# Context keys of the last cross-attention made one layer earlier, subtractions eight tiles ahead, and slot logits multiplied once

## The reference

```python
x_n = l2norm(x_ln, -1) * scale
mu_n = l2norm(mu, 0)
logits = einsum('bnd,des->bnes', x_n, mu_n)
dispatch = softmax(logits, axis=1)
combine = softmax(logits.reshape(B, N, E * S), axis=-1)
slot_in = einsum('bnd,bnes->besd', x_ln, dispatch)
```

```python
q = rope(rms_norm(q, q_norm_w), draft_position_ids)
k = rope(rms_norm(k, k_norm_w), full_position_ids)
scores = einsum('bhqd,bhkd->bhqk', q, repeat(k)) * SCALE
attn = einsum('bhqk,bhkd->bhqd', softmax(scores), v)
```

## Time and profile before

| | |
|---|---|
| three executions | 1602.79, 1604.55, 1605.17 us; median 1604.55 |
| the profiled execution | 1604.83 us, its span 1603.1 us |
| PE busy | 1413.8 us (88%) |
| DVE busy | 1122.8 us (70%) |
| ACT busy | 868.8 us (54%) |
| POOL busy | 469.7 us (29%) |
| mean granted TensorE clock | 0.937 |
| slot experts | 543 to 630 us of the span |
| self-attention of the third layer | 708 to 756 us |
| last cross-attention | 770 to 1238 us |

### The profile page before, as it was taken

How to read it: one execution, slowest core, us unless ns; L and a number is a source line. 1 busy time by engine, 2 the same in 40 slices (tenths; PEclk the granted TensorE clock), 3 DMA queues, 4 the chain that set the end, 5 groups by cost and what they waited for, 6 DMA issues and landing times. The chain is left out here.

```text
span 1603.1 us, 23976 instructions
## 1 busy us (share of the span) xinstructions
PE 1413.8 (88%) x8072; PEld 993.9 (62%) x8072; DVE 1122.8 (70%) x2240; ACT 868.8 (54%) x2300; POOL 469.7 (29%) x515
## 2 busy tenths in 40 slices
PE   7876988867998789987779899999998989999969
PEld 5653444445775457876557677877777436666657
DVE  4687999825665555764559768766854679999953
ACT  2446989832124264426445445445554579999831
POOL 2244000000000001530447326534600037777710
PEclk9986999977999799998889899999999999999979
DMA  3002999965341402200200000000000453333120
GB/s 144 1 1 51 180 185 186 178 183 162 105 136 33 99 14 51 90 1 1 79 2 12 14 8 8 14 1 1 1 1 10 141 159 119 101 103 114 40 78 8
DMA packets 192390, 112.89 MB, mean 70 GB/s; under 512 B 150233, under 2 KB 166617, under 8 KB 191628
## 3 DMA queue, kind: packets, MB, share of 16 engines
q1 hardware_dynamic: 192268, 111.35, 26.7%
HBM read 77.51 MB, written 0.26 MB: 49 GB/s over the span
## 5 line engine op out<-in xcount | busy, mean ns | idle before, releaser
L672 DVE TENSOR_REDUCE x_row_max<-banks 128x1 f32<-128x512 f32 x248 | 152.7, 682 | 14.4 <-PE banks L366 14.3
L575 ACT ACTIVATE x_v_full<-banks,x_neg_max,x_q_scale 128x1024 int16<-128x1024 f32 x128 | 153.4, 1202 | 15.1 <-DMA x_v_full<-x_v_full 7.6
L212 PE MATMUL banks<-a_w_ring,x_normed_T 128*128 128x512 f32 x320 | 146.6, 598 | 4.8 <-DVE a_r L3193 4.8
L2389 PE MATMUL banks<-ctx_tokens,x_kT 128*128 128x512 f32 x272 | 139.8, 601 | 2.4 <-ACT ctx_tokens L2551 2.4
L2416 PEld LDWEIGHTS banks<-x_v,x_weights_T 128*128 128x128 f32 x896 | 111.2, 193 | 30.0 <-ACT x_weights_T L2567 15.9
L2416 PE MATMUL banks<-x_v,x_weights_T 128*128 128x129 f32 x896 | 118.8, 278 | 7.8 <-ACT x_weights_T L2567 7.8
L2505 POOL TENSOR_TENSOR ctx_tokens<-ctx_tokens 128x512 f32<-128x512 f32 (+1 forms) x48 | 71.4, 1487 | 136.6 <-DVE ctx_tokens L2655 136.6
L2674 DVE TENSOR_TENSOR ctx_tokens<-ctx_tokens,x_weights_T 128x512 f32<-128x512 f32 x104 | 88.3, 849 | 31.7 <-ACT x_weights_T L2557 31.2
L366 PE MATMUL banks<-x_kT_parts,x_qT_int 64*128 64x512 bf16 x512 | 103.5, 402 | 7.1 <-DVE x_row_max L672 3.5
L2684 DVE TENSOR_TENSOR x_weights_T<-x_weights_T,ctx_tokens 128x512 f32<-128x512 f32 x112 | 90.2, 829 | 24.8 <-ACT ctx_tokens L2563 24.7
L427 PEld LDWEIGHTS banks<-x_v_full,x_v_int 128*16 128x16 f16 x1024 | 57.2, 91 | 76.3 <-DMA x_v_full<-x_v_full 46.4
(11 more groups left out here) (532 smaller groups left out, 3374.4 us busy)
## 6 DMA issues: line engine op xcount, KB each, us to landing
a_w_ring<-in_L_attn_WB_T SPq DMA_DIRECT2D x16, 512.0 KB
a_w_ring<-in_L_attn_WC_T SPq DMA_DIRECT2D x16, 512.0 KB
f_w_gate_up<-in_L_ffn_gate_up SPq DMA_DIRECT2D x18, 352.0 KB
ctx_tokens<-in_ctx SPq DMA_DIRECT2D x16, 256.0 KB, 5.7
x_wq<-in_L_xattn_Wq_T SPq DMA_DIRECT2D x8, 512.0 KB, 3.7
a_w_ring<-in_L_attn_Wth_T SPq DMA_DIRECT2D x8, 512.0 KB
a_bias_ring<-in_L_attn_B_bias_perm SPq DMA_DIRECT2D x16, 256.0 KB
a_bias_ring<-in_L_attn_C_bias_perm SPq DMA_DIRECT2D x16, 256.0 KB
```

Of the source, the lines that this page charges most:

```text
L212: last = nc.tensor.matmul(out, lhsT, rhs, start=(i == 0), stop=(i == len(pairs) - 1))
L575: nc.scalar.activation(eb[:, q % RING], k.ps[:, 2 + 2 * (q % 2):4 + 2 * (q % 2), :].rearrange("p a n -> p (a n)"), ACT.Exp, bias=nb[:, v % ...
L672: nc.vector.reduce_max(mx[:, u % 2, i:i + 1], k.bank(MBANK[m % 3]), AX.X).then_inc(s.max_taken, 1)
L2389: nc.tensor.matmul(k.bank(s_bank(key)), kt[:, u % 2, j * P:(j + 1) * P], flat(qt[:, u % 2]), start=True, stop=True).then_inc(s.scores_in_p ...
```

## The change

In the slot experts the dispatch logits are no longer a product of their own: TensorE turns tiles of the scaled combine logits (`turn_logits`). Combine logits are therefore made in the order of column pieces, both batch elements of one piece before the next, and from piece 0 ahead of the loop; their exponentials go to a second buffer (`cexp`, in the place of `mu`), both in ScalarE's step 2, and the first products are spread over steps 1 and 2.

```diff
-ncol = sb("neg_mu_rnorm", [P, ne])
+cexp = k.mu[:].rearrange("p c s -> p (c s)").rearrange("p (b s) -> p b s", b=B)
...
     def combine_logits(n):
-        b, j = divmod(n, 4)
+        j, b = divmod(n, B)
+        if b == 0 and j == 0:
+            pe.wait_ge(s.xT_ready, B)
...
-    def dispatch_logits(p):
-        if p == 0:
-            pe.wait_ge(s.xT_ready, B)
-        else:
+    def turn_logits(p):
+        pe.wait_ge(s.logits_taken, B * (p // 2 + 1))
+        if p >= 1:
             pe.wait_ge(s.dexp_ready, 4 * p)
         for e in range(2):
             a = (2 * p + e) * SLOTS
-            last = matmul_acc(nc, k.bank(0, P, BT, e * BT), [(k.mu[:, c, a:a + SLOTS], xst[:, c]) for c in range(DC)])
+            for b in range(B):
+                last = nc.tensor.transpose(k.bank(0, P, P, (e * B + b) * T), comb[:, b, a:a + SLOTS], k.ident[:])
         last.then_inc(s.dlog_ready, 1)
...
         turn_x(b)
-    steps = ((0, dispatch_logits), (1, turn), (3, turn_combine), (2, hidden), (3, slot_out), (4, combine))
+    for n in range(4):
+        combine_logits(n)
+    steps = ((0, turn_logits), (1, turn), (3, turn_combine), (2, hidden), (3, slot_out), (4, combine))
     for i in range(NPAIR + 4):
         for lag, step in steps:
             if 0 <= i - lag < NPAIR:
                 step(i - lag)
-            if lag == 1 and i < 2:
-                for n in range(4 * i, 4 * i + 4):
+            if lag == 0 and i < 2:
+                for n in range(4 + 2 * i, 6 + 2 * i):
                     combine_logits(n)
-            if lag == 1 and i == 1:
-                for n in range(4):
+            if lag == 1 and i in (1, 2):
+                for n in range(2 * i - 2, 2 * i):
                     first_product(n)
...
                 nc.scalar.activation(disp[:, r, e, b], k.bank(0, P, T, (e * B + b) * T), ACT.Exp, bias=dm[:, r, 1, e, b:b + 1],
-                                     scale=k.mu_col[:, 2 * p + e:2 * p + e + 1], accum_out=dm[:, r, 2, e, b:b + 1]).then_inc(s.dexp_ready, 1)
+                                     accum_out=dm[:, r, 2, e, b:b + 1]).then_inc(s.dexp_ready, 1)
 
     def combine_exps(b):
         act.wait_ge(s.cmax_ready, b + 1)
-        nc.scalar.activation(comb[:, b], comb[:, b], ACT.Exp, bias=sm[:, b, 4:5], accum_out=sm[:, b, 5:6]).then_inc(s.cexp_ready, 1)
+        nc.scalar.activation(cexp[:, b], comb[:, b], ACT.Exp, bias=sm[:, b, 4:5], accum_out=sm[:, b, 5:6]).then_inc(s.cexp_ready, 1)
...
-            combine_exps(i - 1)
-        if i == 1:
-            for n in range(4):
+            for n in range(2 * i - 2, 2 * i):
                 take_product(n)
+        if i == 2:
+            for b in range(B):
+                combine_exps(b)
         if i >= 2:
...
                                     b2[:, n % B2R].unsqueeze(1).to_broadcast([P, B, D]), ALU.add).then_inc(s.so_taken, 1)
+    for n in range(4):
+        take_logits(n)
     for i in range(NPAIR + 3):
         if i < NPAIR:
             dispatch_max(i)
         if 0 <= i - 1 < NPAIR:
             take_turned(i - 1)
         if i < 2:
-            for n in range(4 * i, 4 * i + 4):
+            for n in range(4 + 2 * i, 6 + 2 * i):
                 take_logits(n)
```

```diff
 cb = sb("causal", [P, P])
+NK = 4
+k1, k2, ksq = sb("key_cos", [P, NK, NV, HD3]), sb("key_sin", [P, 2, NV, HD3]), sb("key_squares", [P, 2, NV, HD3])
+kst, neg_half = sb("key_rms", [P, NK, 3, NV]), sb("neg_half", [P, NV])
+K_BANKS = (7, V_BANK, V_BANK, V_BANK)
 sm = sb("small", [P, 2, 2, GH])
...
                             channel_multiplier=1).then_inc(s.zeroed, 1)
     pool.wait_ge(s.zeroed, 2)
+
+    def normalise_keys(g):
+        pool.wait_ge(s.key_mults, g + 1)
+        nc.gpsimd.tensor_tensor(k1[:, g], k1[:, g], k2[:, g % 2], ALU.add).then_inc(s.key_added, 1)
+        pool.wait_ge(s.key_ss, g + 1)
+        nc.gpsimd.tensor_scalar(kst[:, g, 1], kst[:, g, 0], 1.0 / HD3, RMS_EPS, ALU.mult, ALU.add).then_inc(s.key_var, 1)
+        pool.wait_ge(s.key_var, g + 1)
+        nc.gpsimd.tensor_tensor(kst[:, g, 2], kst[:, g, 1], neg_half[:], ALU.pow).then_inc(s.key_rstd, 1)
+        pool.wait_ge(s.key_rstd, g + 1)
+        pool.wait_ge(s.key_added, g + 1)
+        nc.gpsimd.tensor_tensor(k1[:, g], k1[:, g], kst[:, g, 2].unsqueeze(2).to_broadcast([P, NV, HD3]), ALU.mult).then_inc(s.key_normed, 1)
+    nc.gpsimd.memset(neg_half[:], -0.5).then_inc(s.pool_step, 1)
+    pool.wait_ge(s.pool_step, 2)
     for j in range(2):
         pool.wait_ge(s.turned, j + 1)
         for b in range(B):
             hs = slice(b * nh, (b + 1) * nh)
             nc.gpsimd.tensor_tensor(pad[:, j, b, :, 0:HD], t1[:, j, hs], t2[:, j, hs], ALU.add).then_inc(s.padded_ready, 1)
+    for g in range(NK):
+        normalise_keys(g)
 
...
     last.then_inc(s.xv_in_psum, 1)
+
+    def project_keys(g):
+        if g == 1:
+            pe.wait_ge(s.xv_taken, 1)
+        if g >= 2:
+            pe.wait_ge(s.key_squared, g)
+            pe.wait_ge(s.keyT_taken, g - 1)
+        for i in range(NV):
+            a = (NV * g + i) * P
+            last = matmul_acc(nc, k.bank(K_BANKS[g], P, HD3, i * HD3), [(k.ctxt[:, c, a:a + P], k.wk3[:, c, 0:HD3]) for c in range(DC)])
+        last.then_inc(s.key_in_psum, 1)
+
+    def turn_keys(g):
+        pe.wait_ge(s.key_normed, g + 1)
+        pe.wait_ge(s.key_squared, min(g + 2, NK))
+        if g:
+            pe.wait_ge(s.keyT_taken, g)
+        for i in range(NV):
+            last = nc.tensor.transpose(k.bank(V_BANK, P, P, i * P), k1[:, g, i], k.ident[:])
+        last.then_inc(s.keyT_in_psum, 1)
+    project_keys(0)
     normalise_pe(k, pe, n_ln)
...
         for b in range(B):
+            if j and b:
+                pe.wait_ge(s.key_squared, 1)
             pe.wait_ge(s.padded_ready, 2 * j + b + 1)
...
 
-    def second_values(u):
-        if u % 2 == 0:
-            pe.wait_ge(s.xv_taken, 1 + u // 2)
-        for i in (2 * u, 2 * u + 1):
-            last = value_tile(1, i, V_BANK)
+    def keys(u):
         if u % 2:
-            last.then_inc(s.xv_in_psum, 1)
+            turn_keys(u // 2)
+        elif u // 2 + 1 < NK:
+            project_keys(u // 2 + 1)
 
...
             scores(u + 2)
-        second_values(u)
+        keys(u)
         if u >= 1:
             weigh(u - 1)
         if u == 6:
...
     def take_values(u, m):
-        act.wait_ge(s.xv_in_psum, u * (m + 1) + 1)
+        act.wait_ge(s.xv_in_psum, 1)
         nc.scalar.copy(k.vt[:, u, NV * m:NV * m + NV, 0:HD3], k.bank(V_BANK).rearrange("p (a n) -> p a n", n=HD3)).then_inc(s.xv_taken, 1)
+
+    def square_keys(g):
+        act.wait_ge(s.key_mults, g + 1)
+        if g >= 2:
+            act.wait_ge(s.key_ss, g - 1)
+        nc.scalar.activation(ksq[:, g % 2].rearrange("p h n -> p (h n)"), k.bank(K_BANKS[g]), ACT.Square).then_inc(s.key_squared, 1)
+
+    def take_keys(g):
+        act.wait_ge(s.keyT_in_psum, g + 1)
+        nc.scalar.copy(k.kt_first[:, NV * g * P:NV * (g + 1) * P], k.bank(V_BANK)).then_inc(s.keyT_taken, 1)
 
     def exps(u):
...
+    square_keys(0)
     for j in range(2):
...
         if u % 2:
-            take_values(1, u // 2)
+            if u // 2 + 1 < NK:
+                square_keys(u // 2 + 1)
+            take_keys(u // 2)
         if u == 6:
             take_attn(0)
...
     normalise_dve(k, dve, n_ln)
+
+    def key_mults(g):
+        dve.wait_ge(s.key_in_psum, g + 1)
+        if g >= 2:
+            dve.wait_ge(s.key_added, g - 1)
+        src = k.bank(K_BANKS[g]).rearrange("p (h n) -> p h n", h=NV)
+        tiles = slice(NV * g, NV * (g + 1))
+        nc.vector.tensor_tensor(k1[:, g], src, k.tc[:, tiles], ALU.mult)
+        for hf in range(2):
+            o = slice(hf * HALF, (hf + 1) * HALF)
+            other = slice((1 - hf) * HALF, (2 - hf) * HALF)
+            last = nc.vector.tensor_tensor(k2[:, g % 2, :, o], src[:, :, other], k.ts[:, tiles, o], ALU.mult)
+        last.then_inc(s.key_mults, 1)
+
+    def key_sums(g):
+        dve.wait_ge(s.key_squared, g + 1)
+        nc.vector.reduce_sum(kst[:, g, 0], ksq[:, g % 2], AX.X).then_inc(s.key_ss, 1)
+    key_mults(0)
     dve.wait_ge(k.w_loaded[7], 160)
...
         maxima(u)
+        if u % 2 == 0 and u and u // 2 < NK:
+            key_mults(u // 2)
+        if u % 2 and u // 2 and u // 2 < NK:
```

```diff
 NW = 4 * 16
-FIRST = (1, 2, 3, 0, 4, 5)
+START = ((1, 1), (0, 0), (0, 5), (1, 2), (1, 3), (1, 4), (1, 0), (1, 5))
+NS = len(START)
+groups = list(START) + [(u, i) for u in range(2, NU) for i in range(NGR)]
 PROJECT_AT = (0, 2, 4, 6, 8, 10)
 TURN_AT = (5, 7, 9, 11, 13, 15)
-PROJECT_AT_0 = (0, 3, 6, 9, 12, 15)
-TURN_AT_0 = (9, 12, 15)
-AHEAD_SHIFT, AHEAD_EXP = 3, 2
+PROJECT_AT_0 = {1: 4, 5: 5, 9: 6, 13: 7}
+TURN_AT_0 = {4: 3, 6: 2, 8: 4, 12: 5}
+AHEAD_SHIFT, AHEAD_EXP = 8, 4
 S_BANKS, O_BANKS, K_BANK, TURN_BANK, M_BANK = (0, 1, 2), (3, 4), 5, 6, 7
 old = k.swap_pools()
 n_ln = k.n
...
 
-EARLY = 2
+EARLY = 1
 
...
 
 def group_bank(u, i):
-    return K_BANK if u else (3, 4, 5, 2)[at(0, i) % 4]
```

(57 more changed lines are left out.)

127 lines of the change are left out of this document (59 added, 68 removed).

## The result

The changed kernel took 1581.08 us (median of 4 runs, 1579.63 to 1586.09), the kernel before beside it 1604.46 (1602.79 to 1605.17): ratio 0.9861, 95% interval 0.9838 to 0.9884. That is 23.4 us less where I forecast 27, inside the range. The profiled execution took 1586.09 us, 18.7 less than the one of before (1604.83).

What follows compares the result with a forecast made beforehand. Steady units were taken as bound by TensorE, the start and first unit as holding idle and low-clock time. Terms -4 + 5 - 18 - 1.5 - 3.5 - 5 gave -27, so 1577.5 us; range 1564 to 1591.

Steps and rivals of the forecast that it cites:

- slot experts: Slot experts' stage: dispatch logits no longer multiplied a second time, steps of 5.1 instead of 6.19 us; -4 us.
- cross-attention, to the first score: Start of the last cross-attention: queries second in line, two places earlier, so the first score comes sooner; -5.5 us.
- first unit's loop and change: Cross-attention's first unit and change to the second: moved values cost +7.2, removed waits and idle give -8.7; -1.5 us.
- second unit: Cross-attention's second unit: idle time before its turning, half-clock work and two waits go, 1.5 given back; -3.5 us.
- steady units and end: Units three to six: exponential waits (4 x 0.7) and output-projection idle at unit changes (6 x 0.4) go; -5 us.
- I take 0.7 for the start: Start of the slot experts' stage gains only 0.7 us, as both combine exponentials stand before the fourth dispatch.
- I take +1.1 for each of three pairs: Self-attention's loop: key groups, turnings and waits for squares add 1.1 us per pair of steps.
- rival (b): Slower, 1612 us: new waits and subtractions leave TensorE below full rate for long in the later units; chance 0.04.
- The risk from GpSimd in the self-attention: Self-attention: new GpSimd work might slow VectorE's 16 score passes, up to 5.5 us; forecast that 0 falls due.
- Now 17 scores ... 26.5: Cross-attention's start: first score to turned maxima takes 26.5 us instead of 36.0, so -9.5.
- rival (a): Under half the gain, 1593 us: GpSimd's and VectorE's chain paces the 17 scores, self-attention costs 10; chance 0.16.
- no idle row above 2: Sign of being right: no TensorE idle row above 2 us at the cross-attention's second unit's turning.

Runs made afterwards that it cites:

- bank_and_order: Changed kernel with three of four self-attention key groups projected into an idle bank and keys turned behind the weighing of values; 1581.43 us.
- spare_in_attn: Changed kernel with eight spare 128-column identity turnings before each of the eight turnings of exponentials in the self-attention, all waits kept; 1580.08 us.
- slots_alone: Kernel before with only the edits of the slot experts' stage and what feeds it; 1598.46 us, ratio 0.9953.
- ahead_alone: Kernel before with only eight tiles subtracted and four exponentiated ahead, and the last value group before the output projection; 1595.24 us, ratio 0.9931.
- without_ahead: Changed kernel with three tiles subtracted and two exponentiated ahead again, last value group still before the output projection; 1589.25 us.
- squares_later: Changed kernel with ScalarE squaring each projected group one score copy later among the first unit's 17 scores; 1574.76 us, ratio 0.9810.
- scalar_scales: Changed kernel with the last four of eight groups at the cross-attention's start scaled by ScalarE instead of GpSimd; 1581.49 us.

## Why the prediction was right, and where its terms were off

By the profiled executions (us), with the units counted from first weighing to first weighing as in the earlier trace rows:

| term | forecast | measured |
|---|---|---|
| slot experts | -4 | -7.2 |
| self-attention, its start | +1.6 | +1.45 |
| self-attention, its loop | +3.3 | +11.8 |
| cross-attention, to the first score | -5.5 | -5.8 |
| first score to turned maxima | -9.5 | -6.7 |
| turned maxima to first weighing | -3 | -1.8 |
| first unit's loop and change | -1.5 | -1.0 |
| second unit | -3.5 | -1.9 |
| steady units and end | -5 | -6.2 |
| sum | -27 | -17.3 |

- **Slot experts.** The steps came as forecast: 6.19 to 4.90, though TensorE without a gap paces them, not ScalarE. Mis-sized was "I take 0.7 for the start". From the first turning of the stage (545.80; 544.01 after) to the first combine (594.19; 589.10) it is 48.4 before and 45.1 after, 3.3 less. Five dispatch products go there as well, 11.5 us in all (the first took 3.78 at the low level), for five turnings of 3.6; of these 7.9 us 4.6 came back as waits and slow passes.
- **Self-attention.** This is the step that failed: "I take +1.1 for each of three pairs". The term measured +13.2, outside even its bound of +10. Two of the three waits were sized right, 0.8 each; the first was 1.30. What was missing is that TensorE falls to its low level behind the second and the third of them: of 11.7 us in the loop, 8.9 are 221 passes running longer (35.8 against 26.9), and 2.9 are waiting. Pairs of steps took 7.3 us from 727.85 and 9.8 from 735.18, where I had 6.7. bank_and_order and spare_in_attn show it from two sides. I had the clock as rival (b), but put it into the later units, where nothing fell: the first unit stands at 0.93 (0.89 before), the second and the steady ones at 1.00. The Trainium skill, "TensorE: Matmul & The Clock Gate", section "HAM oscillation — how this bites in real kernels", describes bursts that each start at half rate because a wait for a DMA longer than the burst stands in front. The waits here, 0.8 to 1.3, are shorter than the work between them, so that case does not foretell them. The trace has the same direction: 0.66 with these waits, 0.95 with spare work around them.
- **The risk from GpSimd in the self-attention** (up to 5.5) did not fall due: VectorE's passes on scores took 0.69 beside GpSimd's 1.02 and 1.04 (rows of both below). The Trainium skill, "SBUF — State Buffer", section "Who interferes with whom", had it so. Its other half, that GpSimd shuts out a VectorE operation with two SBUF inputs, shows in the cross-attention's maxima: beside GpSimd's passes on 128x512 1.48 becomes 2.16 and 3.04.
- **Start of the cross-attention.** The two places in the queue are worth 5.8, and the low clock at its beginning is as I took it. "Now 17 scores ... 26.5" counted TensorE's work; the pace was the hand-over of copies and squares between VectorE and ScalarE, with GpSimd beside it. TensorE had done its last score by 813 and waited 4.22 for VectorE. That is close to the mechanism of rival (a), at some 40% of its price (14.3 gained of 18, where (a) left 9). The sum of (a) was itself off: two thirds of the terms outside the start and the self-attention (14) are 9, not 13, so its case was some 1596; nothing else in the forecast hangs on it.
- **Units.** The exponentials' waits went in every unit as forecast. Idle times of 2.08 and 2.49 stayed at the changes into units two and three; "no idle row above 2" was wrong by a little there, and the second unit's gain with it. Counted from maxima to maxima instead, the second unit grew by 1.4 us (58.0 to 59.4) and the third shrank by 3.0 (56.3 to 53.3), so the row of the second unit depends on the marks.
- **Total.** Against the forecast the self-attention is 8.4 longer, the cross-attention's start 3.7, its first two units 2.1; the slot experts are 3.2 shorter and the steady units 1.2. The traced gain is 17.3, the medians' 20 to 23. Of the difference 1.9 lies in the rest of the first profile; the traces are all of the changed kernel's slower group, and what the faster one does is not shown. So a median within 4 us of the forecast is in part luck: terms were off by 8.4, 3.7 and 2.1 us one way and by 3.2 and 1.2 the other, and the median came out nearer to the forecast than the traced sum.
- **The keys by themselves.** No run has their move alone. By difference of stretches it brought little: 17.3 less the 8.7 of slots_alone and the 11.0 of ahead_alone leaves a loss of 2.4, and less 7.2 for the slot experts and the 6.3 that without_ahead gives back, a gain of 3.8. The 14.3 gained at the cross-attention's start are mostly paid for by 13.2 in the self-attention and by the values that moved into the first unit.

The first dispatch product of the kernel before:

```profile
549.48 3.78 PE L212 MATMUL banks<-f_x_l_T,mu 128*128 128x256 f32 x8 [0.46 <-ACT f_x_l_T L1393]
```

VectorE and then GpSimd in the changed kernel's self-attention:

```profile
728.99 0.69 DVE L2068 SCALAR_TENSOR_TENSOR ctx_tokens<-banks,a_causal 128x512 f32<-128x512 f32 x1 [1.08 <-PE banks L1915]
```

```profile
728.28 1.02 POOL L1846 TENSOR_TENSOR a_key_rms<-a_key_rms,a_neg_half 128x4 f32<-128x4 f32 x1
729.38 1.04 POOL L1849 TENSOR_TENSOR a_key_cos<-a_key_cos,a_key_rms 128x512 f32<-128x512 f32 x1
```

## What to carry to other kernels

Before a wait is priced, look at what TensorE does around it: in this stage of short bursts, three waits of 0.8 to 1.3 us came with 8.9 us of slower passes, and with spare work packed around the same waits the loop was 5.4 us shorter, the spare work included. Distances that let the exponentials run ahead took a change of two numbers and paid in every unit. Where one engine's copies stand in order behind an operation that waits for another engine, look at the order first: moving that operation by one place gave 1.5 us here, while giving the copying engine a third engine's work cost 1.1.

## What the runs showed of the hardware that I had not expected

- Work that nothing needs made the stage shorter: 56 spare 128-column turnings in the loop, and it took 37.96 us instead of 43.34.
- Contention between VectorE and GpSimd runs both ways, down to tiny passes: GpSimd's power on 128x4 took 1.54 beside the maxima and 1.02 alone. With VectorE's idle time gone, two maxima beside GpSimd grew from 2.16 to 3.04 us.
- Stages that no edit touches differ by up to 10 us between executions of nearly the same program (875.9 in squares_later, 886.0 in scalar_scales), while the changed kernel's stretch of 706 us repeated to 0.2 in three profiles.
